# A two-layer post-norm transformer on one core: the layer norm's last step on ScalarE, one maximum instruction for two heads, and layer 1's ternary weights made early, in pieces, as int8

## The reference

```python
x = L0_attn_x                                         # (4, 256, 256) f32
x = _layernorm(x + _L0_attn_ref(x, w_project, w_out))         # q, k, v, causal softmax, w_out
x = _layernorm(x + _L0_ffn_ref(x, ...))   # silu(x@gate*gate_s) * (x@up*up_s) @ down * down_s, inner 704
x = _layernorm(x + _L1_attn_ref(x, Wq, bq, Wk, bk, Wv, bv, Wo, bo))
x = _layernorm(x + _L1_ffn_ref(x, W_up, W_gate, W_down))      # inner 1024
# the weights of the last one are made ternary first:
scale = jnp.mean(jnp.abs(w)) + 1e-08
q = jnp.clip(jnp.round(w / scale), -1.0, 1.0) * scale
```

## Time and profile before

| | us |
|---|---|
| median of 3 runs (268.95 to 269.27) | 269.2 |
| the profiled execution | 269.13 |
| its span, first to last instruction | 267.4 |
| TensorE busy (matmul) | 248.4 |
| TensorE weight loads busy | 222.9 |
| VectorE busy | 211.8 |
| GpSimd busy | 159.2 |
| ScalarE busy | 153.9 |

### The profile page before, as it was taken

One profiled execution on the slowest core, in us unless ns is written; L12 is line 12 of the kernel. 1 busy time (PEld: TensorE's weight loads), 2 busy tenths in 40 slices (PEclk: granted clock), 3 DMA queues, 4 the chain that ended last, 5 costly groups with the idle time before them and its releaser, 6 DMA issues.

```text
span 267.4 us, 6860 instructions
## 1 busy us (share of the span) xinstructions
PE 248.4 (93%) x2502; PEld 222.9 (83%) x2502; DVE 211.8 (79%) x688; ACT 153.9 (58%) x284; POOL 159.2 (60%) x176
## 2 busy tenths in 40 slices
PE   8789779999999999999999979989999999999990
PEld 7689757777898999889999878576689788999980
DVE  2466999858678955859899988999999884988574
ACT  3576228799643166955545268887585764434430
POOL 8767247789613145822562799839924894626361
PEclk9999999999999999999999999999999999999997
DMA  5998762762000004426400035670130000010102
GB/s 163 287 260 207 206 182 89 199 174 84 2 0 4 1 4 115 123 72 167 157 2 0 6 84 157 214 182 4 25 137 4 2 1 2 0 42 0 42 1 78
DMA packets 20146, 23.26 MB, mean 87 GB/s; under 512 B 2833, under 2 KB 17681, under 8 KB 19729
## 3 DMA queue, kind: packets, MB, share of 16 engines
q1 hardware_dynamic: 19968, 22.56, 29.9%
q10 hardware_dynamic: 144, 0.26, 0.3%
HBM read 9.05 MB, written 1.05 MB: 38 GB/s over the span
## 4 chain that ended last, share of the span: by engine, by line
PE 64%; DVE 13%; DMA 6%; issue 5%; POOL 4%; ACT 3%; SPq 3%; POOLq 0%; DVEq 0%; ACTq 0%
PE pair L524 10%; PE pair L525 9%; PE pair L526 9%; PE pair L700 6%; PE pair L701 5%; PE pair L631 4%; DVE block_max L947 4%; PE pair L614 4%; DMA raw<-a 2%; PE pair L592 2%; PE pair L641 2%; PE pair L724 2%; PE pair L725 2%; PE pair L634 2%; SPq L499 2%
## 5 line engine op out<-in xcount | busy, mean ns | idle before, releaser
L1131 POOL TENSOR_TENSOR hidden<-hf,hidden 128x512 fp32r<-128x512 f32 x28 | 36.2, 1294 | 41.0 <-ACT hidden L836 40.9
L794 ACT ACTIVATE probs<-pair 128x768 f32<-128x768 f32 x64 | 49.5, 813 | 13.9 <-PE pair L616 6.9
L1115 POOL TENSOR_SCALAR_AFFINE_SELECT probs<-probs 128x512 f32<-128x512 f32 x64 | 44.7, 712 | 16.6 <-ACT probs L794 16.0
L955 DVE CUSTOM_DVE_ANT_0 masked<-pair,mask 128x256 bf16<-128x256 f32 x80 | 33.4, 417 | 2.0 <-PE pair L593 1.8
L614 PE MATMUL pair<-q_stack,k_stack 98*128 98x256 bf16 x128 | 26.5, 274 | 4.5 <-ACT probs L794 2.2
L836 ACT ACTIVATE hidden<-hf 128x512 fp32r<-128x512 f32 x28 | 17.7, 630 | 16.4 <-DVE hf L1034 11.7
L1024 DVE SCALAR_TENSOR_TENSOR hf<-th,pair 128x512 f32<-128x512 f32 x28 | 19.1, 683 | 8.7 <-ACT th L828 4.9
L524 PE MATMUL pair<-xT_hi,gu_hi 128*128 128x256 f32 x88 | 25.5, 289 | 0.0
L525 PE MATMUL pair<-xT_lo,gu_hi 128*128 128x256 f32 x88 | 24.9, 283 | 0.0
L526 PE MATMUL pair<-xT_hi,gu_lo 128*128 128x256 f32 x88 | 24.9, 283 | 0.0
L616 PE MATMUL pair<-q_stack,k_stack 98*128 98x128 bf16 x128 | 23.7, 218 | 0.0
(11 more groups left out here) (156 smaller groups left out, 898.2 us busy)
## 6 DMA issues: line engine op xcount, KB each, us to landing
q_stack<-q_part SPq DMA_DIRECT2D x48, 128.0 KB, 2.7
k_stack<-k_part SPq DMA_DIRECT2D x48, 128.0 KB, 2.7
raw<-f SPq DMA_DIRECT2D x3, 1024.0 KB, 4.9
raw<-a SPq DMA_DIRECT2D x8, 256.0 KB, 3.7
raw<-f0gu SPq DMA_DIRECT2D x4, 352.0 KB, 3.5
x<-x_nat SPq DMA_DIRECT2D x4, 256.0 KB, 5.8
out<-x SPq DMA_DIRECT2D x4, 256.0 KB, 2.4
raw<-f0dn SPq DMA_DIRECT2D x3, 256.0 KB, 3.4
```

What stands on the lines that cost most here:

```text
L794: nc.scalar.activation(probs[(n - 1) % 4][:, :, :], place(key)[:, :, 0:T + P], ACT.Exp, scale=SC).then_inc(exp_done, 1)
L955: nc.vector.tensor_tensor_reduce(out=masked[:, j, 0:T], in0=o[:, 0:T], in1=mask[:, 0:T], scale=1.0, scalar=NEG, op0=ALU.add, op1=ALU.max, ...
L1115: pool.affine_select(out=diag, in_=diag, compare_op=ALU.is_ge, fill=0.0, base=0, pattern=[[0, 2], [0, 2], [1, P]], channel_multiplier=-1). ...
L1131: pool.tensor_tensor(hidden[(n - 1) % NHID][1][:, :, :], hf[n % 2][:, :].rearrange("p (a t) -> p a t", a=2), hidden[(n - 1) % NHID][0][:, ...
```

## The change

- The last step of the layer norm goes from VectorE to ScalarE, as `Identity(res * rstd + offset)`, two instructions for a batch. For it VectorE negates the mean (one more small instruction in `residual`) and GpSimd multiplies it by `rstd` (`offset`, one more small instruction behind the power, with a semaphore between them). VectorE waits before it reuses `res` until ScalarE has read it.
- The block maxima of a step's two heads (first three batches) are one `tensor_reduce` over both PSUM banks, which starts when both heads' scores are there and frees both banks at once.
- The ternary step is cut up. `raw` is filled through two slots of 2 KB on each partition (pieces listed in `PIECES`), and every piece of layer 1's feed-forward weights is loaded twice: 12 pieces for `AB` (ScalarE's sums of |w|), 12 for `TERN` (thresholding). `TS` is the sum over partitions. Gate and up (`TERN` 0 to 7) are made in layer 0 and staged as int8 in the unused half of `raw`; when layer 0's last `GU` is done, ScalarE copies them into place (`CV`, eight instructions). Down (`TERN` 8 to 11) is written directly.
- All five tables and `BANKS` are new. PSUM is one tensor of 8 banks, so that two heads may lie in banks that aren't neighbours. The number of matmuls is unchanged.

```diff
+PIECES = ([("PREP0", n) for n in range(PREP0)] + [("PREP1", n) for n in range(3)] + [("AB", n) for n in range(12)]
+          + [("TERN", n) for n in range(8)] + [("PREP1", 3)] + [("TERN", n) for n in range(8, 12)])
+CONVERTED = (0, 4, 1, 5, 2, 6, 3, 7)
 TENSOR_STEPS = """
-    QK:000-1 XI:010 XI:020 XI:030 V:000 V:010 V:020 QK:010-1 QK:020-1 S:000-2 QK:030 S:003-5 QK:031 S:006-7
+    QK:000-1 XI:010 XI:020 XI:030 V:000 V:010 QK:010-1 QK:020-1 S:000-3 QK:030 S:004-5 QK:031 S:006-7 V:020
...
+        staged = raw[:, 1024:2048].bitcast(mybir.dt.int8)
...
SP:
+                    elif i < PREP0 or i >= PREP0 + 2:
+                        sp.wait_ge(*raw_used(PIECES[i - 2]))
...
+                        m, c = columns_of(n)
+                        sp.dma_start(raw_of(PIECES[i], 512), f1[:, m, c]).then_inc(landed, 16)
TensorE:
-                            pe.wait_ge(tern_done, 8)
+                            pe.wait_ge(converted, 4)
+                    if l == 1 and b == 0 and i == 2:
+                        pe.wait_ge(converted, 8)
ScalarE:
+                if step == "LN":
+                    n = nth("LN", l, b)
+                    act.wait_ge(rstd_done, n)
+                    for tt in range(TT):
+                        last = nc.scalar.activation(x[:, TT * b + tt, :], res[n % 2][:, tt, :], ACT.Identity,
+                                                    scale=rstd[n % 2][:, tt:tt + 1], bias=offset[n % 2][:, tt:tt + 1])
+                    last.then_inc(ln_done, 1)
...
+                if step == "AB":
+                    act.wait_ge(*raw_landed(("AB", i)))
...
+                if step == "CV":
+                    n = CONVERTED[i]
+                    m, c = columns_of(n)
+                    act.wait_ge(tern_done, n + 1)
+                    act.wait_ge(gu_mm, nth("GU", 0, NB - 1, MT0 // 2 - 1))
+                    nc.scalar.activation((gu_hi, gu_lo)[m][:, c], staged[:, 512 * n:512 * (n + 1)], ACT.Copy).then_inc(converted, 1)
VectorE:
+                if n > 2:
+                    dve.wait_ge(ln_done, n - 2)
...
+                nc.vector.tensor_scalar(mv[k_][:, :, 0], mv[k_][:, :, 0], -1.0, None, ALU.mult)
                 nc.vector.tensor_scalar(mv[k_][:, :, 1], mv[k_][:, :, 1], EPS, None, ALU.add).then_inc(var_done, 1)
...
+                    if nb_of(l, b) < MASKED_BY_PE:
+                        dve.wait_ge(s_mm, 2 * nth("S", l, b, i))
+                        nc.vector.tensor_reduce(block_max[b % 2][:, 2 * i:2 * i + 2, 1:4],
+                                                both(key)[:, :, 0:3 * P].rearrange("p j (c t) -> p j c t", t=P),
+                                                mybir.AxisListType.X, ALU.max).then_inc(max_taken, 2)
+                        continue
...
-                        ins = nc.vector.tensor_scalar(x[:, TT * b + tt, :], res[n % 2][:, tt, :], mv[n % 2][:, tt, 0:1],
-                                                      rstd[n % 2][:, tt:tt + 1], ALU.subtract, ALU.mult)
...
GpSimd:
-                    pool.tensor_tensor(rstd[n % 2][:, :], mv[n % 2][:, :, 1], minus_half[:, :], ALU.pow).then_inc(rstd_done, 1)
+                    pool.tensor_tensor(rstd[n % 2][:, :], mv[n % 2][:, :, 1], minus_half[:, :], ALU.pow).then_inc(power_done, 1)
+                    pool.wait_ge(power_done, n)
+                    pool.tensor_tensor(offset[n % 2][:, :], mv[n % 2][:, :, 0], rstd[n % 2][:, :], ALU.mult).then_inc(rstd_done, 1)
```

More of the change, by code:

```diff
@@ L281, in program @@
         rstd = [sb(f"rstd{n}", [P, TT]) for n in range(2)]
+        offset = [sb(f"offset{n}", [P, TT]) for n in range(2)]
         minus_half = sb("minus_half", [P, TT])
@@ L291, in program @@
         abs_sum = sb("abs_sum", [P, 3, 4])
[L292 to L295, removed]
-        out_gain = sb("out_gain", [P, 1])
-        pairs = [ctx.enter_context(nc.psum_tensor(f"pair{n}", [P, 2, 512], fp32)) for n in range(4)]
+        of_matrix = sb("of_matrix", [P, 15])
+        scale, half, minus, total, out_gain = (of_matrix[:, n:n + 3] for n in (0, 3, 6, 9, 12))
+        psum = ctx.enter_context(nc.psum_tensor("psum", [P, 8, 512], fp32))
         x_in = [sem(f"x_in{n}") for n in range(NB)]
@@ L376, in last_reader @@
                     "CB": (shift_done, n), "S": (max_taken, 2 * n - 1 + k), "ST": (exp_done, n), "GU": (hf_done, n),
-                    "TERN": (thresholds, i // TERN + 1)}[kind]
-        takers = [q for q in order if not (q[0] == "D" and q[3]) and not (q[0] == "TERN" and q[3] % TERN != 1)]
+                    "TS": (thresholds, n)}[kind]
+        takers = [q for q in order if not (q[0] == "D" and q[3])]
         banks_of = {q: [tuple(int(n) for n in part) for part in taken.split("+")] for q, taken in zip(takers, BANKS.split(), strict=True)}
+        banks_of.update({q: sorted(c) for q, c in banks_of.items() if q[0] == "S"})
         before, held = {}, {}
@@ L390, in place, with both @@
             c = banks_of[step[:3] + (0,) if step[0] == "D" else step][k]
-            return pairs[c[0] // 2] if len(c) == 2 else pairs[c[0] // 2][:, c[0] % 2, :]
+            return psum[:, c[0]:c[0] + 2, :] if len(c) == 2 else psum[:, c[0], :]
+        def both(step):
+            (lo,), (hi,) = banks_of[step]
+            return psum[:, lo:hi + 1:hi - lo, :]
         def first_x(b):
@@ L539, in _ @@
             for _ in range(WARM):
-                nc.tensor.matmul(pairs[3][:, 1, 0:P], ones[:, :], ones[:, :], start=True, stop=True)
+                nc.tensor.matmul(psum[:, 7, 0:P], ones[:, :], ones[:, :], start=True, stop=True)
             for step, l, b, i in order:
@@ L726, in _ @@
                     last.then_inc(d_mm, 1)
-                if step == "TERN" and i % TERN == 1:
-                    m = i // TERN
-                    pe.wait_ge(abs_done, 4 * (m + 1))
-                    nc.tensor.matmul(take(key)[:, 0:4], ones[:, :], abs_sum[:, m, :],
+                if step == "TS":
+                    pe.wait_ge(abs_done, 4 * (i + 1))
+                    nc.tensor.matmul(take(key)[:, 0:4], ones[:, :], abs_sum[:, i, :],
                                      start=True, stop=True).then_inc(sum_mm, 1)
```

238 lines of the change are left out of this document (112 added, 126 removed), and 16 rows, old and new, of the table BANKS.

## The result

The changed kernel took 271.91 us (median of four runs, 271.38 to 273.31) against 269.07 for the kernel before beside it: a ratio of 1.0116, 95% interval 1.0075 to 1.0158. A second series, of six executions, gave 1.0081 (1.0052 to 1.011). It is slower, by about 1%. The forecast was 264.0, with a range of 257.5 to 269.5. Some executions run slower at a lower granted clock (the profiled one with the maxima split shows 0.91 from 40 to 60 us); the ratios leave out those that count as slow, and spans are used only for where time goes.

The account below looks back on a forecast made before the run. TensorE was taken as fed in most stretches, with 20.6 us of weight-load waits winnable by new tables and a lighter VectorE. Sum: 269.1 - 1.3 - 5.5 + 0.5 + 1.2 = 264.0 us, range 257.5 to 269.5.

Parts of the forecast that it names:

- Layer 1's attention, -5.5 us: 146 to 217 us: VectorE, busy 66.3 of 71 us, gets lighter, so the stretch shrinks 5.5 us; bounds 0 and 11.2.
- The first rival: Layer 1's attention: held by the chain from maxima to PV, so relief doesn't reach TensorE; 268.5 us, chance 0.19.
- 40 to 146 us, +0.5 us: Layer 0 and start of layer 1: moved ternary work and norms hide behind TensorE's work except 0.5 us; bounds -3, +3.
- the one place where a norm looked late: At XT:100, thinnest cover found: 4.6 us of TensorE work beside a 4.5 to 5.8 us chain; 0.5 us taken.
- The bound of +3: 40 to 146 us: upper bound in us on what the moved work could cost there.
- The wait that I looked for, for the norm's x: TensorE's waits for the norm's x, expected to be not above 1.5 us in all.
- the two signs that were to show the prediction wrong: Over 3 us added waits for x or thresholds before 146 us; or layer 1's attention keeping 11 us with lighter VectorE.
- The first batches, -1.3 us: 28 to 40 us: earlier key DMAs and merged maxima at 0.88 us a step gain 1.3 us; bounds 0 and 4.0.
- the lower bound, 0: 28 to 40 us: the smallest gain allowed for the first batches, 0 us.
- The tail, +1.2 us: Behind the last product: negation 0.17, GpSimd's multiply 0.72, ScalarE's pair 0.3 lengthen it; bounds 0.5 and 1.8.
- The third rival: Norms before XT: each of 12 chains 1.2 us longer, eight exposed stop in-order TensorE; 273.1 us, chance 0.14.

## Why the prediction was wrong

**Layer 1's attention, -5.5 us, for a lighter VectorE: this step failed.** Standing time from 140 to 200 us fell by 3.4 us and the waits from 146 to 217 by 5.1, so the size was not far off. But the argument was that VectorE, at 93% of the stretch, held it. With VectorE at 60.83 us in the old order standing time fell by only 0.8, and in the new tables with the norm back on VectorE and small ternary work nearly all of the gain is there. So by far the most of the 3.4 comes with the new order of steps and not with the lighter engine. That the size came out near the forecast is luck. The first rival named this mechanism (the relief does not reach TensorE) and should have had more than 0.19: the earlier trace rows named exponentials and masks.

**40 to 146 us, +0.5 us: this step failed, and it decides the result.** It put 7 us on VectorE, 15 on ScalarE and 12.5 on GpSimd where weight loads filled 90%, and priced only the one place where a norm looked late. Standing time rose by 3.7 us from 60 to 140 us and by 0.8 from 40 to 60. Making the ternary work small gave back 1.9 of the 3.7 and 0.8% of the time. But the new tables bring the rise by themselves too, with the norm back and the ternary work small (within 0.4 us of the changed kernel's standing time), and for a new order the sum had no term. Nor was ScalarE as full as forecast: it was busy for 71.5 of the 106 us, where the prediction counted 88. The bound of +3 was too low: it was drawn from idle time of each engine over the stretch, and an in-order engine that is idle on average is not idle when its next result is wanted. The wait that I looked for, for the norm's x, is 0.3 us here. Neither of the two signs that were to show the prediction wrong came (3 us of waits for x or thresholds, 11 us of waits left in layer 1's attention): they watched single waits, and the loss was spread over many.

**The first batches, -1.3 us: 0 came of it.** The keys' wait of 1.50 us is gone, though the first `S` came 1.05 us earlier and not 1.5. The 0.88 us for a merged maximum was right, and so was the lead of the first `ST`, 1.15 us for 1.0 to 1.1. But standing time in the first 40 us is the same (7.5 for 7.6). The next three `ST` steps stand directly behind the first in the new order, and each waited for a bank that batch 1's maxima still held (0.27, 0.38 and 0.38 us idle before their matmuls). The old order puts a step of `S` between the second and the third, and between the third and the fourth. That both heads' banks come free together is not the reason, since the split maxima gave waits as long. I had taken the gain at the start as a gain at the end; the lower bound, 0, was the measured value.

**The tail, +1.2 us: 0.6.** The mis-sized term is GpSimd's multiply, 0.19 us for 128x2 where I took the power's 0.69 for the same shape: from the power's start to the last step's it is 1.00 us, 0.28 more than before, where 0.72 was counted. The negation added 0.08 us, not 0.17, as the eps behind it starts before it ends (264.45, 264.53). The pair on ScalarE took 1.09 where I took 1.05. An estimate from the figures of the Trainium skill ("ScalarE: Activation LUTs", section "What ACT_TABLE_LOAD costs") is 1.08, and the trace agrees within 1%.

**From 200 us to the last product** the sum had no term, and standing time rose by 0.6 us there; the longest wait is 0.9 us for the norm's x, where there was none before. With the norm back on VectorE it is still 0.7, so it comes mostly with the order.

**The third rival** had the direction and, at 273.1 us, nearly the size, but not the mechanism for this kernel. Its price is real in the old tables (+2.1%), and the new tables absorb it: the norm's return changes nothing there, and ScalarE waits 10.6 us for the offset where it waited 23.6.

What the runs give, step by step from the kernel before: ternary work made small in its old place -0.2%; new tables, merged maxima and two-slot loads +0.8; norm to ScalarE -0.5; ternary work whole again, at its new place, +0.8 to 1.1. That is +0.8 to 1.2% in all, and it must be, since each step starts where the last one ended. The parts don't stand by themselves: with the norm on VectorE the ternary work at its new place costs 0.4% (1.0097 for 1.0059, give or take 0.4), and then the norm's move nothing. So the new tables cost 0.8%, and the norm and the ternary work together, less what the latter cost in its old place, 0 to 0.4%. Why the tables cost it stays open: order, loads and PSUM banks were not tried apart.

## What to carry to other kernels

A busy share of 93% does not say that an engine holds the stretch: before crediting a lighter engine, look at what the waiting engine's waits end on, and shrink that work in place to see if the time follows. A new order has a price of its own: run it with the moved work made small, beside the old order with the same work made small. Work moved into a stretch where TensorE seems fed has a price even if each engine keeps idle time, since engines that run in order lend their lateness to everything behind; price such a move by what stands behind each moved instruction. A step that depends on a long chain over several engines belongs on an engine whose queue can spare the wait: in the old tables the norm on ScalarE was too early in one place and too late in the next.

## What the runs showed that was not expected

On GpSimd a power and a multiply over the same 128x2 elements differ almost fourfold (groups of the changed kernel: busy, mean ns):

```profile
L1142 POOL TENSOR_TENSOR rstd<-mv,minus_half 128x2 f32<-128x2 f32 x16 | 11.7, 730 | 13.7 <-DVE mv L925 13.7
L1144 POOL TENSOR_TENSOR offset<-mv,rstd 128x2 f32<-128x2 f32 x16 | 3.1, 195 | 1.3
```

And the negation on VectorE, 0.17 us at the quiet end, takes 309 ns in the mean of its 16:

```profile
L924 DVE TENSOR_SCALAR mv<-mv 128x2 f32<-128x2 f32 x16 | 5.0, 309 | 0.5
```

In the kernel with the last norms on VectorE the same kind of instruction took 0.35 us at 263.38, while GpSimd was at work, and 0.17 at the end. The Trainium skill ("GPSIMD Engine Reference", section "1. Specifications") says that GpSimd shares its SBUF interfaces with VectorE and contends with its instructions in a two-port mode or with two SBUF inputs. That would fit if the negation ran in such a mode, which no trace here shows; the runs show that the two go together, not why.
